# First row maxima of three narrow attentions from float32 features instead of stacked bf16 pieces

## The reference

```python
s = einsum("bhld,bhsd->bhls", q, k) / sqrt(8)     # 16 heads, d = 8
o = softmax(s, axis=-1) @ v
y = o.reshape(b, 256, 128) @ W_out + bias
```

## Time and profile before

| | us |
|---|---|
| median of 3 runs (2190.03 to 2192.88) | 2192.5 |
| the profiled execution | 2194.88 |
| its span, first to last instruction | 2193.1 |
| PE busy | 1875.5 |
| DVE busy | 1522.1 |
| ACT busy | 1299.4 |
| POOL busy | 588.4 |

### The profile page before, as it was taken

The page is one execution under the profiler, slowest core; times in us unless marked ns, Lnnn a source line. Parts: engine busy times, 40 slices in busy tenths (PEclk is TensorE's granted clock), DMA queues, the critical chain, the costliest instruction groups (busy, mean ns, idle before and its releaser), DMA issues.

```text
span 2193.1 us, 37675 instructions
## 1 busy us (share of the span) xinstructions
PE 1875.5 (86%) x13296; PEld 1246.2 (57%) x13296; DVE 1522.1 (69%) x3631; ACT 1299.4 (59%) x2773; POOL 588.4 (27%) x569
## 2 busy tenths in 40 slices
PE   7999775997999999967987488999997997679896
PEld 5777562445777777632444255566665676434465
DVE  5777675875767777647847848899997457568553
ACT  5777532775887888734765746776665222347632
POOL 3223003202544443414101003444443001121035
PEclk9999895998999999977988699999999898779898
DMA  4000003421000000005402000000000100254012
GB/s 201 1 1 2 1 1 115 134 61 39 1 1 1 1 1 1 1 13 173 124 1 79 0 1 1 1 1 1 1 1 20 40 1 1 113 158 135 26 50 88
DMA packets 80154, 87.38 MB, mean 40 GB/s; under 512 B 6578, under 2 KB 70115, under 8 KB 79073
## 3 DMA queue, kind: packets, MB, share of 16 engines
q1 hardware_dynamic: 78625, 82.49, 12.0%
q0 software_dynamic: 1344, 2.49, 0.4%
HBM read 54.39 MB, written 30.70 MB: 39 GB/s over the span
## 4 chain that ended last, share of the span: by engine, by line
PE 54%; DVE 28%; ACT 7%; issue 5%; POOL 3%; DMA 2%; SPq 0%; DVEq 0%; POOLq 0%; ACTq 0%
PE bank L469 45%; DVE scratch L1221 5%; PE bank L653 2%; ACT XN L1996 2%; DVE scratch L3071 2%; PE bank L368 2%; DVE scratch L3091 2%; PE bank L2953 2%; PE bank L693 1%; DVE stats L245 1%; DVE XN L3111 1%; DVE scratch L1608 1%; DVE w_keep L1895 1%; ACT L2074 1%; PE bank L1190 1%
## 5 line engine op out<-in xcount | busy, mean ns | idle before, releaser
L469 PE MATMUL bank<-scratch 64*128 64x256 bf16 (+7 forms) x3056 | 340.3, 307 | 67.3 <-DMA scratch<-parts 39.3
L1221 DVE TENSOR_REDUCE scratch<-bank 128x2 f32<-128x512 f32 x384 | 244.6, 686 | 82.3 <-PE bank L469 79.7
L469 PEld LDWEIGHTS bank<-scratch 64*128 64x128 bf16 (+4 forms) x3056 | 184.0, 122 | 195.6 <-DVE scratch L1221 73.9
L469 PE MATMUL bank<-w_keep,scratch 128*128 128x128 f32 (+4 forms) x1760 | 243.6, 329 | 19.3 <-DVE scratch L1938 4.1
L1307 ACT ACTIVATE w_keep<-bank 128x512 f32<-128x512 f32 x384 | 212.5, 597 | 52.0 <-PE bank L469 44.3
L469 PE MATMUL bank<-XNT,w_keep 128*128 128x256 f32 (+4 forms) x800 | 237.7, 436 | 4.6 <-POOL w_keep L2135 2.4
L469 PEld LDWEIGHTS bank<-w_keep,scratch 128*128 128x128 f32 (+3 forms) x1760 | 182.2, 184 | 84.0 <-issue 55.0
L469 PEld LDWEIGHTS bank<-XNT,w_keep 128*128 128x128 f32 x800 | 149.5, 196 | 57.2 <-issue 28.6
L469 PE MATMUL bank<-w_early,scratch 64*128 64x256 f32 (+3 forms) x1152 | 161.8, 343 | 18.0 <-ACT w_early L3171 8.9
L469 PEld LDWEIGHTS bank<-w_early,scratch 64*128 64x128 f32 (+3 forms) x1152 | 117.9, 183 | 62.6 <-issue 21.8
L469 PE MATMUL bank<-w_keep 128*32 128x256 f32 (+1 forms) x1600 | 124.2, 386 | 11.2 <-ACT w_keep L1307 5.4
(11 more groups left out here) (451 smaller groups left out, 3778.7 us busy)
## 6 DMA issues: line engine op xcount, KB each, us to landing
scratch<-parts SPq DMA_DIRECT2D x24, 1024.0 KB, 5.0
parts<-scratch SPq DMA_DIRECT2D x192, 96.0 KB, 2.4
parts<-scratch SPq DMA_DIRECT2D x96, 64.0 KB, 2.1
w_early<-pack_l3f SPq DMA_DIRECT2D x1, 5206.0 KB, 14.8
w_keep<-pack_l2f SPq DMA_DIRECT2D x1, 2124.0 KB, 12.6
w_early<-pack_mamba SPq DMA_DIRECT2D x1, 2120.0 KB, 18.7
w_keep<-pack_l2x SPq DMA_DIRECT2D x1, 2049.0 KB, 7.9
w_keep<-taps SPq DMA_DIRECT2D x4, 512.0 KB, 5.1
```

Of the source, the lines that this page charges most:

```text
L469: return pe.matmul(out, lhsT, rhs, start=start, stop=stop, skip_group_check=True)
L1221: dve.tensor_reduce(neg[:, :, h], self.k.bank[5 - g % 2][:, :].rearrange("p (t s) -> p t s", s=S), AXX, ALU.max, negate=True).then_inc(*s. ...
```

## The change

For the 16 heads of batch 0 the raw scores are no longer made from the stack but from the float32 features. A head's 8 features lie among the 64 of its half, so ACT first makes eight masked copies of the queries (`mask_act`): copy w keeps the features of pair w and sets the others to zero, by an activation whose scale is a column of 0 and 1. They lie in buffers of the exponentials, which are free until step 0. PE then multiplies 64 rows of masked queries with 64 rows of keys in float32. The wait on stack 0 moves to step 0. The maximum alone comes from these products; the scores that are weighed are made from the stack as before.

Three things go with it. Project 1 is put into bank 6 and waits for no copy; project 0 waits for the first quarter of its input alone, and the wait for the other quarters moves to project 2 (in the raw attention there is nothing to project, and its PE still waits for all quarters). POOL leaves the features of the first batches uncut in place and puts the rest elsewhere (`level`, `residue`). And batch 1's twelve writes are shared: ACT issues the eight of the pieces 0 and 1 after it has copied project 1, SP issues the last four directly behind batch 0's twelve and ahead of the load of stack 0. The semaphore of the writes is split into one for each DRAM buffer.

```diff
     AHEAD = 10
+    DIRECT = 16
...
+    def sources(self, b):
+        at = slice(b * S, (b + 1) * S)
+        if self.projection is None:
+            return self.qsrc[:, at], self.ksrc[:, at]
+        return self.level(b)[:, 0:S], self.level(b)[:, S:2 * S]
+    def level(self, b):
+        return self.expo[4] if b == 0 else self.flat[b % 2]
+    def residue(self, b):
+        return self.expo[5 + b] if b < 2 and self.projection is not None else self.flat[b % 2]
+    def masked(self, b, w):
+        if b == 0:
+            return self.expo[w // 2][:, w % 2 * S:(w % 2 + 1) * S]
...
-        if compares and x % H == 0:
+        direct = x < self.DIRECT
+        if compares and (x == self.DIRECT or x % H == 0 and not direct):
             pe.wait_ge(*s.loaded_stack(x // H % 3).at(x // H))
+        if compares and direct:
+            pe.wait_ge(*s.lowered.at("masked", x // H, x % H // 2))
...
-                    m = mm(pe, k.bank[4 + i][:, c * S:(c + 1) * S], self.head(0, y)[:, c * P:(c + 1) * P], self.head(1, y))
+                    queries, keys = self.head(0, y), self.head(1, y)
+                    if direct:
+                        rows = slice(HW * (y % 2), HW * (y % 2 + 1))
+                        queries, keys = self.masked(y // H, y % H // 2)[rows, :], self.sources(y // H)[1][rows, :]
+                    m = mm(pe, k.bank[4 + i][:, c * S:(c + 1) * S], queries[:, c * P:(c + 1) * P], keys)
...
+    def project_bank(self, b):
+        return self.k.bank[6 if b == 1 else 7]
...
-        self.emptied(pe, p)
+        if (kind, b) != ("project", 1):
+            self.emptied(pe, p)
         if kind == "project":
+            for q in {0: (0,), 2: (1, 2, 3)}.get(b, ()):
+                pe.wait_ge(*self.turned_at(q))
+            bank = self.project_bank(b)
...
+            if p in (self.FIRST, self.FIRST + H // 2):
+                self.mask_act(act, (p - self.FIRST) // (H // 2))
+            if p == self.FIRST + H // 2:
+                for c in range(2):
+                    self.spread(act, 1, c)
+    def mask_act(self, act, b):
...
+        for w in range((min(self.DIRECT, (b + 1) * H) - b * H) // 2):
+            act.activation(self.masked(b, w), queries, ACT.Identity, scale=self.k.w["same_d"][:, w:w + 1]).then_inc(*s.lowered.up("masked", b, w))
...
-            for c, made in enumerate((0, 2, 3)):
...
+            if b != 1:
+                for c in range(3):
+                    self.spread(sp, b, c)
+            if b == 0:
+                for c in range(2, 3):
+                    self.spread(sp, 1, c)
             if b >= 3:
                 sp.wait_ge(*s.scored.at("s", (b - 2) * H - 1))
-            sp.wait_ge(*s.parts_out.at(b))
+            sp.wait_ge(*s.parts_out[b % 2].at(b))
```

More of the change, by code:

```diff
@@ L1318, in act @@
                     act.wait_ge(*s.pool.at("cut", b - 2, 3))
+                if b == 3:
+                    act.wait_ge(*s.compared.at("x", self.DIRECT - 2))
                 for n in range(2):
-                    a = act.activation(self.flat[b % 2][:, n * S:(n + 1) * S], k.bank[7][:, n * S:(n + 1) * S], ACT.Identity,
+                    a = act.activation(self.level(b)[:, n * S:(n + 1) * S], self.project_bank(b)[:, n * S:(n + 1) * S], ACT.Identity,
                                        bias=self.projection[2 + n])
@@ L1332, in act @@
                 act.activation(self.negt[b % 3], k.bank[7][:, :].bitcast(BF16)[:, 0:S], ACT.Copy).then_inc(*s.flip_s.up(kind, b))
+            if p in (self.FIRST, self.FIRST + H // 2):
[4 more added lines that the diff above has]
+    def mask_act(self, act, b):
+        s, queries = self.k.s, self.sources(b)[0]
+        if self.projection is not None:
+            act.wait_ge(*s.stacked.at("project", b))
+        for w in range((min(self.DIRECT, (b + 1) * H) - b * H) // 2):
+            act.activation(self.masked(b, w), queries, ACT.Identity, scale=self.k.w["same_d"][:, w:w + 1]).then_inc(*s.lowered.up("masked", b, w))
     def preset_pool(self, pool):
@@ L1354, in cut_pool @@
             pool.wait_ge(*at(0))
-            pool.tensor_tensor(fl, fl, self.part(b, 0), ALU.subtract).then_inc(*up(1))
+            pool.tensor_tensor(rest, fl, self.part(b, 0), ALU.subtract).then_inc(*up(1))
         else:
@@ L1382, in bias_pool, with spread @@
         pool.tensor_tensor(tiles, tiles, bias_bc.unsqueeze(1).to_broadcast([P, 4, D]), ALU.add).then_inc(*self.k.s.preset.up("bias", q))
+    def spread(self, e, b, c):
+        s, dram, wide = self.k.s, self.k.parts_dram[b % 2], H // 2 * S
+        e.wait_ge(*s.pool.at("cut", b, (0, 2, 3)[c]))
+        for n, parts in enumerate((QUERY_PARTS, KEY_PARTS)):
+            among = [j for j in range(HD) if parts[j] == c]
+            for o in range(2):
+                row = n * P + o * HW + among[0] * HD
+                place = bass.AP(dram.tensor, dram.offset + row * wide, [[S, HW], [(among[1] - among[0]) * HD * wide, len(among)], [1, S]])
+                part = self.part(b, c)[o * HW:(o + 1) * HW, n * S:(n + 1) * S].unsqueeze(1).to_broadcast([HW, len(among), S])
+                e.dma_start(place, part).then_inc(*s.parts_out[b % 2].up(*((b,) if (c, n, o) == (2, 1, 1) else (b, c, n, o))))
     def sync(self, sp):
@@ L1465, in pe @@
         pre_norm_pe(k, e)
-        all_flat(k, e, "pre")
         core.pe(e)
@@ L1508, in pe @@
         turn_pe(k, e, "rms", lambda i: O[:, i, :], lambda i: normed(k, "rms", i))
-        for q in range(QUARTERS):
-            e.wait_ge(*s.formed.at("scaled", q))
         core.pe(e)
```

34 lines of the change are left out of this document (15 added, 19 removed).

## The result

The changed kernel takes 2180.52 us (median of 5 runs, 2178.9 to 2185.4) beside 2192.88 us for the kernel before in the same session (2190.03 to 2196.8): a ratio of 0.9942, 95% interval 0.9928 to 0.9956, or 12.4 us less. The forecast was 2183.0. The profiled execution took 2180.52 us, with a span of 2178.7 and a mean granted clock of 0.933; before it was 2193.1 and 0.921.

A forecast was written before the change was run, and what follows sets the result against it. The prediction took the wait on the stack's writes and load at the head of each narrow attention as the bound; hybrid 5.8 + guarded 5.8 - raw 2.0 = 9.6 us off the 2192.5 median gave 2183 us, range 2171 to 2190.

The forecast's parts named there:

- The wait on the stack: Head of each narrow attention: TensorE's wait on the stack's DMA falls from 39 us to near zero.
- The price of a pair: Batch 0's comparisons: a float32 pair of heads costs 1.91 us at full clock, 2.86 at half, against 1.39 with bf16.
- that rival: Float32 pairs: the two lanes don't overlap, a cold pair costs about 3.5 us; 2195, or 2207 at half clock everywhere; chance 0.06.
- Hybrid, 5.8 forecast: Hybrid attention: full clock before the stall, half clock for the last four pairs, mark at 370.7 instead of 376.52, gain 5.8 us.
- the wait of 3 us: Hybrid, ahead of value 0: PE idles 3 us because ACT's copy of project 2 stands behind its DMA writes.
- the mark: Each narrow attention: start of DVE's L1236, cutting batch 0's finished maxima; what moves it was taken to move the stage.
- Guarded, 5.8 forecast: Guarded attention: value 0 done at 1923.1, then four half-clock pairs, mark at 1935.1 against 1941.02, gain 5.8 us.
- Raw, -2.0 forecast: Raw attention: comparisons start ten us earlier but run at half clock throughout, mark at 1009.6, 2.0 us later than 1007.68.
- The rival at twice that price: ACT issues a write at twice SP's 0.66 us, stall grows 5.3 us in two attentions: 2193.5, no change; chance 0.08.
- Covered by 2 to 5 us: Hybrid: stack 1 lands at 365.5, or 368 if loads share bandwidth, 2 to 5 us before batch 1's comparisons need it.
- half clock everywhere: Every comparison at half clock: gains 3.8 hybrid, 3.1 guarded, -2.0 raw, sum 4.9 us, 2187.6; chance 0.22.
- full clock in more places: Full clock also after the stall and in raw: 26 us, 2166.5, or 2171 to 2178 with one or two hot; chance 0.18.

The follow-up runs named there:

- the run with the warm-up: Changed kernel plus six extra 128x256 float32 matmuls, their result unread, ahead of the raw stage's comparisons: 2175.54 us.
- project 2 apart: Changed kernel with project 2 in bank 3 instead of bank 7, so value 0 no longer waits for project 2's copy: 2175.49 us.
- four banks as well: Changed kernel with both: direct pairs alternating between banks 4, 5 and 0, 1, and project 2 in bank 3: 2166.00 us.
- four banks: Changed kernel with direct pairs alternating between banks 4, 5 and banks 0, 1: 23.0 us faster than the kernel before the change.

## Why the prediction held

**The wait on the stack.** Right: of 39.3 us one wait of 0.5 is left. The first comparisons come 10.5, 10.5 and 10.2 us into their stages, where 10.6, 10.5 and 10.3 were forecast.

**The price of a pair.** 1.91 and 2.86 us were forecast, 1.97 and 2.92 measured; the 2.11 us for the eight records at half clock, taken from a 128-row chain, were 2.08. The lanes overlap, so that rival falls.

**Hybrid, 5.8 forecast, 9.1 measured.** Pairs 0 and 1 ran at full clock, as taken, but 0.9 us late, since the sum left out that VectorE was still normalizing. From pair 2 on the forecast had the clock the wrong way round. Pair 2, project 2 and pair 3 ran at half clock and filled the time until ScalarE's copy, so that the wait of 3 us was missing, and that nearly unbroken work (6.66 of 7 us) was followed by a rise to full clock for the last four pairs, where half had been taken. Pair 4's place was nearly right (358.7 forecast; measured at 360.5 with the stage starting 1.5 us later), by luck: slower pairs and no wait made up for one another. From there to the mark it took 8.4 us where 12.0 were forecast, which less 0.3 us of later start is the surplus of 3.3.

Nor is that order fixed. In the run with the warm-up, whose hybrid stage has the same instructions, pairs 0 to 3 ran at full clock, TensorE then waited ahead of value 0 as forecast, and the clock fell behind the wait (1.00 until 361 us, 0.54 in 361 to 369):

```profile
356.54 0.71 PE L469 MATMUL bank<-w_early,scratch 128*128 128x128 f32 x4 [2.39 <-ACT scratch L1357]
```

Its mark is at 32.30 us, a gain of 7.95. So the forecast's course occurs, and costs about 1 us more than the other. What decides between the two was not tested.

**Guarded, 5.8 forecast, 6.5 measured.** Every step was in its place: the first comparison 10.2 us into the stage (10.3 forecast), full clock ahead of the wait, a wait of 3.0 us on ScalarE's copy, half clock behind it. That the gain comes within 0.7 us says less: over the four executions of this stage it is 5.1 to 6.5. At the end of the stage 5.4 us are left; the 1.1 us that go after the mark were not traced.

**Raw, -2.0 forecast, -2.4 at the mark and -3.0 at the end.** Half clock throughout, as taken. Two terms were missing: that the cut would now fall on GpSimd's pieces for a later batch (0.75 us), and that the shared writes alone would cost the stage 3 us if it compared from the stack. The prediction counted SP's four more issues ahead of stack 0 and gave them no price; in this kernel that holds, since nothing waits for stack 0 there, but they are not free in themselves.

**ScalarE's writes.** 0.72 and 0.70 us each (5.79 for eight in the hybrid stage, 5.56 in the guarded) against 0.66 taken from SP. The rival at twice that price falls.

**Stack 1.** "Covered by 2 to 5 us" was too much: forecast at 365.5 or 368, it was first used at 368.60, with a stage that began 1.5 us later, so the second value, for two loads that share bandwidth, was the better. With the last hybrid pairs at full clock it was waited for by 0.5 us, and it is the first thing late in the hybrid and guarded stages of most of what was tried beyond (4.15 us with project 2 apart, 19.4 with four banks as well).

**The clock.** Neither rival on it came true as a whole: half clock everywhere is refuted by 1.97 us pairs, full clock in more places came true for four pairs of one stage. The sum 5.8 + 5.8 - 2.0 = 9.6 was 9.1 + 6.5 - 2.4 = 13.2 at the marks and 11.3 at the stages' ends. That the median moved by 12.4 and stayed 2.5 us from the forecast owes something to chance: at the stages' ends 3.2 us more than forecast in the hybrid stage stood against 1.0 less in the raw one and 0.4 less in the guarded one.

## What to carry to other kernels

A price by the piece is not enough where consumer and producer take turns on one buffer: here 1.1 us of matmuls and 1.3 us of maxima cost 2.9 us, because the turn adds the two, and because in the raw stage the clock, at half when the pairs began, did not rise while there were such pauses. Look for a second pair of banks before counting on faster instructions, and after each gain look up what is late next: it was the stack, then value 0's wait on a copy behind DMA issues, then stack 1. Parts of a change can be worth nothing or less alone and more than their sum together, so test them singly and in pairs, and stage by stage. And look at what a moved stage now stands beside: small VectorE operations took up to 2.2 us more because they met GpSimd's work.

## What the hardware showed that I had not expected

**Small VectorE operations beside GpSimd.** The cut's five operations take 0.19 us each with GpSimd idle, and a cast among them 0.94 us (the changed kernel) and 1.03 (the raw stage from the stack) beside GpSimd's L1419, each time ending within 0.1 us of a GpSimd instruction's end; a subtraction with two inputs took 1.19 in the raw stage with four banks, ending 0.05 us after a GpSimd instruction. Not every one is hit: a subtraction that began together with L1419 (997.64, raw stage from the stack) took 0.19; the maxima in between, which read a bank, keep their 0.69 (686 ns is their mean on the page). The Trainium skill has it so (SBUF — State Buffer, "Who interferes with whom"): casts (in modes with two ports) and operations with two SBUF inputs contend with GpSimd for one pair of ports, which is locked exclusively, and `tensor_reduce` never does. The traces agree: 0.94 and 1.03 us beside a GpSimd instruction of 1.15 and 1.21, and 0.69 for the maxima.

**DMA issues overtake activations.** In the raw stage ScalarE's queue issues its first write at 975.77, while eight masks that stand ahead of it in the program run until 979.1: issues and activations interleave. The eight masks end 3.28 us after their start, as they do in the run with the direct comparisons only, where no writes are on ScalarE's queue.

**Two stack loads at once.** Stack 1's load, issued at 361.0 directly behind stack 0's (359.37), was there for the comparison at 368.60, and the longest of the 24 loads took 7.5 us from issue to landing, where the median is 5.0 and the longest before was 5.6. That the two loads share bandwidth was not tested apart from the writes that run beside them. The view of that line:

```profile
DMA to landing us min/median/max: 4.8/5.0/7.5
```

**TensorE's clock and 64-row work.** At half clock the raw stage kept TensorE busy 20.3 of 24 us without a rise; with four banks the same 64-row matmuls ran without any pause from 976.33 and the granted clock was 1.00 from 982 on.
